# The seam between the key/value stage and the attention loop: an earlier first query chain, with memory of its own and doubly staged weights

## The reference, cut to what matters

```python
# layer 1: cross attention over 16 batches of 128 rows, width 512, 16 query heads, 4 key/value heads of 128
q = layernorm(x) @ Wq + bq ;  k = ctx @ Wk + bk ;  v = ctx @ Wv + bv
q = rmsnorm(q) * qn_w      ;  k = rmsnorm(k) * kn_w           # per head
probs = softmax(q @ k.T / sqrt(128) + mask)                    # each key head serves 4 query heads
x = x + (probs @ v) @ Wo
# layer 2: routed FFN. The best 16 of each batch's 128 rows by a router score are gathered,
# pass an attention block and an MLP, and are scattered back, gated
x = x + ffn(layernorm(x))
```

## Time and profile before

| | |
|---|---|
| median of 3 runs | 876.07 us (873.81 to 878.23) |
| profiled execution, its own time | 879.73 us |
| its span, first to last instruction | 878.0 us |
| TensorE busy | 820.9 us, 93% |
| VectorE, ScalarE, GpSimd busy | 66%, 54%, 53% |
| mean granted TensorE clock | 0.977 of full speed |
| transfers | 81.37 MB, 93 GB/s over the span |
| TensorE waiting in 107 to 155 us | seven waits of 0.76 to 3.74 us |

### The profile page before, as it was taken

One profiled execution on the slowest core, in us unless ns is written; L12 is line 12 of the kernel. 1 busy time (PEld: TensorE's weight loads), 2 busy tenths in 40 slices (PEclk: granted clock), 3 DMA queues, 4 the chain that ended last, 5 costly groups with the idle time before them and its releaser, 6 DMA issues. The chain is left out here.

```text
span 878.0 us, 14307 instructions
## 1 busy us (share of the span) xinstructions
PE 820.9 (93%) x4216; PEld 683.7 (78%) x4216; DVE 577.5 (66%) x1049; ACT 474.0 (54%) x1620; POOL 464.0 (53%) x485
## 2 busy tenths in 40 slices
PE   6999958999999999999999999999987799978997
PEld 4888836888888888888888888888875677766786
DVE  4454445677777777777777777777677588663513
ACT  4555534565566566566566566566554256553431
POOL 2333324555555555555555555555557196644980
PEclk9999997999999999999999999999998699999999
DMA  6566654011111111111111111111024565303520
GB/s 206 202 203 204 202 180 135 13 61 36 48 60 36 48 60 36 48 60 36 48 60 36 48 60 36 48 60 36 24 90 140 213 182 178 118 29 117 192 97 24
DMA packets 49287, 81.37 MB, mean 93 GB/s; under 512 B 4144, under 2 KB 12464, under 8 KB 49264
## 3 DMA queue, kind: packets, MB, share of 16 engines
q1 hardware_dynamic: 48688, 79.25, 27.5%
q0 software_dynamic: 576, 1.84, 0.6%
HBM read 63.77 MB, written 17.30 MB: 92 GB/s over the span
## 5 line engine op out<-in xcount | busy, mean ns | idle before, releaser
L1002 ACT ACTIVATE sq_junk<-q_row 128x128 bf16<-128x128 f32 x256 | 76.0, 298 | 159.6 <-DVE q_row L1256 159.6
L849 POOL TENSOR_TENSOR wp_lo<-raw,wp_hi 128x2048 fp32r<-128x2048 f32 (+1 forms) x24 | 105.0, 4385 | 45.3 <-ACT wp_hi L914 45.2
L1010 ACT ACTIVATE p_row<-s_row,neg_max 128x128 f32<-128x128 f32 x256 | 99.9, 392 | 37.0 <-DVE neg_max L1277 36.4
L1656 PE MATMUL b_y<-wo_hi,oT_hi 128*128 128x512 f32 x256 | 107.1, 419 | 1.0 <-DVE oT_lo L1187 1.0
L1656 PE MATMUL b_q<-wq_hi,xT_hi 128*128 128x512 f32 x252 | 105.6, 419 | 2.2 <-DVE k_row L1210 2.2
L780 POOL TENSOR_TENSOR p_row<-p_row,p_inv 128x512 f32<-128x512 f32 x64 | 66.6, 1041 | 66.7 <-DVE p_inv L1286 66.7
L1658 PE MATMUL b_y<-wo_hi,oT_lo 128*128 128x512 f32 x256 | 101.7, 397 | 0.0
L1657 PE MATMUL b_y<-wo_lo,oT_hi 128*128 128x512 f32 x256 | 101.6, 397 | 0.0
L1658 PE MATMUL b_q<-wq_hi,xT_lo 128*128 128x512 f32 x252 | 99.7, 396 | 0.0
L1657 PE MATMUL b_q<-wq_lo,xT_hi 128*128 128x512 f32 x252 | 99.6, 395 | 0.0
L738 POOL TENSOR_TENSOR q_rs<-q_ss,eps_head 128x4 f32<-128x4 f32 x64 | 12.7, 199 | 153.8 <-ACT sq_junk L1002 153.8
(11 more groups left out here) (298 smaller groups left out, 2266.0 us busy)
## 6 DMA issues: line engine op xcount, KB each, us to landing
cx<-in_ctx_dram SPq DMA_DIRECT2D x16, 256.0 KB, 2.6
wq_raw<-in_L_xattn_Wq_dram SPq DMA_DIRECT2D x16, 256.0 KB, 2.8
wo_raw<-in_L_xattn_Wo_dram SPq DMA_DIRECT2D x16, 256.0 KB, 3.1
v_store<-v_out SPq DMA_DIRECT2D x16, 256.0 KB, 3.3
k_store<-k_out SPq DMA_DIRECT2D x16, 256.0 KB, 2.0
xr<-in_x_dram SPq DMA_DIRECT2D x16, 256.0 KB, 2.7
k_raw<-k_store SPq DMA_DIRECT2D x16, 256.0 KB, 2.6
v_raw<-v_store SPq DMA_DIRECT2D x16, 256.0 KB, 2.8
```

Source lines behind the costliest of these rows:

```text
L849: pool.tensor_tensor(wp_lo[n % NSLOT][:, part, :], raw[RAW_OF[n]][:, part, :], wp_hi[n % NSLOT][:, part, :].bitcast(fp32), ALU.subtract).t ...
L1002: sq = act.activation(sq_junk[:, h, :], q_row[:, h, :], ACT.Square, accum_out=q_ss[:, h:h + 1])
L1010: e = act.activation(p_row[:, h, :], s_row[:, h, :], ACT.Exp, bias=neg_max[:, h:h + 1], accum_out=p_sum[:, h:h + 1])
L1656: pe.matmul(dst, left[0], right[0], start=start, stop=False)
```

## The change

What it does, engine by engine:

- Memory: the query rows, their squares buffer and sums, and `q_nrm` get room of their own, outside what is laid over; the squares of the keys share that buffer; two FFN tiles (`proj`) are put in `q_row` and `q_nrm`. The weight buffers become two slices each of `raw[0]` and `raw[1]`, so two heads can be staged.
- SyncE: loads of head b+1 are issued in batch b, head 0 and 1 both in batch 0, after the splits of Wk and Wv that free the slices. x of batch 0 is loaded in batch 13, not 14. The first quad's bias is issued after the last key projection; then the stores of batch 14, the rest of the query bias, and after the last value projection keys 0, mask, values 0, x of batch 1, residual, last stores. The loop of the queue is written out.
- TensorE: x is turned ahead of key projection 15, query 0 is projected (into `b_y`) between keys 15 and values 15; then keys 15 are turned (into `b_pT`) and quad 1 is projected into `b_q`. In the loop's first batch quad 2 is projected behind scores 0 (into `b_y`), quad 3 behind the turn of quad 1, and the turn of quad 2 has no projection behind it.
- VectorE: statistics of x ahead of the last context split; x normalised between key rows 14 and value rows 14; bias of query 0 between key rows 15 and the low halves of head 15, which now stand ahead of value rows 15; bias 1 before the loop, together with waits for the whole query bias and the mask; bias 2 behind the maxima of quad 0.
- ScalarE: squares of query 0 behind the weighing of keys 14, ahead of the copies of head 15; values 0 copied before the exponentials of quad 0.
- GpSimd: root of x's statistics ahead of keys 14; norm of query 0 right behind keys 15.

```diff
@@ -177,6 +177,13 @@
         f_ms = sb_in(ctx, "f_ms", [P, 2 * NJ])
         f_rs = sb_in(ctx, "f_rs", [P, 2 * NJ])
         raw = [sb_in(ctx, f"raw{i}", [P, 4, W]) for i in range(2)]
+        q_row = sb_in(ctx, "q_row", [P, QUAD, HD])
+        q_nrm = sb_in(ctx, "q_nrm", [P, QUAD, HD])
+        sq_junk = sb_in(ctx, "sq_junk", [P, QUAD, HD], bf16)
+        q_ss = sb_in(ctx, "q_ss", [P, QUAD])
+        q_rs = sb_in(ctx, "q_rs", [P, QUAD])
+        wq_raw = [raw[0][:, i, :].rearrange("p (c d) -> p c d", c=DC) for i in range(2)]
+        wo_raw = [raw[1][:, i, :] for i in range(2)]
 
 
...
@@ -263,7 +262,7 @@
             rope = [sb_in(st, "rope0", [P, 4 * (HD // 2)])]
             onehot = sb_in(st, "onehot", [P, NB, PICK])
 
-            proj = [sb_in(st, f"proj{i}", [P, W]) for i in range(2)]
...
+            def load_x(b):
+                sp.dma_start(xr[:], x_rows[bass.ds(b * S, S), :]).then_inc(x_loaded, 16)
+
+            for b in range(NB - 1):
+                if b < NB - 2:
                     sp.wait_ge(c_turned, b + 1)
-                    sp.dma_start(cx[par][:], ctx_rows[bass.ds((b + 2) * S, S), :]
-                                 ).then_inc(cx_loaded[par], 16)
-
-                wait(sp, w_lo, 2 * b)
-                sp.dma_start(wq_raw[:], chunked(Wq)[:, :, bass.ds(b * HD, HD)]).then_inc(wq_loaded, 16)
-                sp.dma_start(wo_raw[:], Wo[bass.ds(b * P, P), :]).then_inc(wo_loaded, 16)
-                if beside is not None:
-                    beside()
-                if not first:
+                    sp.dma_start(cx[b % 2][:], ctx_rows[(b + 2) * S:(b + 3) * S, :]
+                                 ).then_inc(cx_loaded[b % 2], 16)
+                if b == 0:
+                    load_weights(0)
+                load_weights(b + 1)
+                if b == NB - 3:
+
+                    sp.wait_ge(c_turned, NB - 1)
+                    load_x(0)
+                if b > 0:
                     store_v(b - 1)
                     store_k(b - 1)
...
+            key_weights_over(sp)
+            spread(bq_row[:, 0:W], bq[0:W]).then_inc(first_bias_loaded, 16)
+            store_v(NB - 2)
+            store_k(NB - 2)
+            spread(bq_row[:, W:NH * HD], bq[W:NH * HD]).then_inc(kv_bias_loaded, 16)
...
-            sp.wait_ge(k_stored, 16 * (NB - 1))
-            sp.wait_ge(v_stored, 16 * (NB - 1))
+            sp.wait_ge(k_stored, 16 * (NB - 2))
+            sp.wait_ge(v_stored, 16 * (NB - 2))
+            weights_over(sp)
             load_k(0)
+            sp.dma_start(mask[:], attn_mask.rearrange("a s t -> (a s) t")).then_inc(const_loaded, 16)
             load_v(0)
-            spread(bq_row[:, W:NH * HD], bq[W:NH * HD]).then_inc(kv_bias_loaded, 16)
-            sp.dma_start(x_res[:], x_rows[0:S, :]).then_inc(res_loaded, 16)
-
             sp.wait_ge(x_normed, 1)
             load_x(1)
+            sp.dma_start(x_res[:], x_rows[0:S, :]).then_inc(res_loaded, 16)
             store_v(NB - 1)
             store_k(NB - 1)
...
-            with pool.Fori(0, NB - 1) as b:
+            with pool.Fori(0, NB - 2) as b:
                 kv_batch(b)
 
             def x_norm_stat(b):
@@ -790,11 +787,10 @@
 
 
             x_norm_stat(0)
+            kv_batch(NB - 2)
             kv_batch(NB - 1)
-
-            pool.wait_ge(w_lo, 2 * NB)
+            q_norm(0)
             weights_over(pool)
-            q_norm(0)
             k_low(0)
...
+            def kv_batch(b, par, nth, first, last):
+                if not last:
+                    turn_c(b + 1, 1 - par)
+                act.wait_ge(k_biased, b + 1)
+                wait(act, k_rooted, b)
+                for h in range(NKV):
+                    sq = act.activation(sq_junk[:, h, :], k_row[:, h, :], ACT.Square, accum_out=k_ss[:, h:h + 1])
+                sq.then_inc(k_squared, 1)
+                if not first:
+                    weigh_k(b - 1)
+                if last:
+                    act.wait_ge(k_squared, NB)
+                    squares(0)
+                act.wait_ge(head_loaded[par], 32 * nth)
+                copy(wq_hi[:, :, bass.ds(b * HD, HD)], wq_raw[par]).then_inc(w_hi, 1)
+                copy(wo_hi[:, bass.ds(b, 1), :], wo_raw[par].unsqueeze(1)).then_inc(w_hi, 1)
+
+            kv_batch(0, 0, 1, True, False)
+            with act.Fori(0, NB // 2 - 1) as g:
+                kv_batch(2 * g + 1, 1, g + 1, False, False)
+                kv_batch(2 * g + 2, 0, g + 2, False, False)
...
+            weigh_k(NB - 1, b_pT)
             weights_over(act)
-            weigh_k(NB - 1)
-            squares(0)
             k_high(0)
...
+                    if first and i == 0:
+                        v_high(0)
...
+            x_statistics(0)
+            dve.wait_ge(x_stats, 1)
+            x_moments(0)
+
+            turn_c(NB - 1, 1)
+            key_rows(NB - 2)
+            dve.wait_ge(c_turned, NB)
+            x_norm(0)
+            value_rows(NB - 2)
+            x_low(0)
+            weights_low(NB - 2, 0)
+
+            key_rows(NB - 1)
+            dve.wait_ge(first_bias_loaded, 16)
+            q_bias(0, 0, b_y)
+            weights_low(NB - 1, 1)
+            value_rows(NB - 1)
             weights_over(dve)
-
-            dve.wait_ge(w_lo, 2 * NB)
-            dve.wait_ge(rows_loaded, 32)
-            q_bias(0, 0)
-
             dve.wait_ge(kv_bias_loaded, 48)
+            q_bias(1, 1)
+            dve.wait_ge(const_loaded, 64)
...
-                        q_bias(1, 1, b_y)
                         q_low(0)
...
                     if not (first and i == 0) and not (last and i == NQUAD - 1):
-                        q_bias(t + 1, (i + 1) % NQUAD)
+                        if not (first and i == 1):
+                            q_bias(t + 1, (i + 1) % NQUAD)
                     s_mask(t)
                     s_sum(t)
                     s_max(t)
+                    if first and i == 0:
+                        q_bias(2, 2, b_y)
                     if not (first and i == 0):
                         p_low(t - 1)
...
-            def kv_batch(b, par, next_nth, first=False, last=False):
-                if not last:
+            def kv_batch(b, par, next_nth, first=False, between=None):
...
                 if not first:
                     turn_k(b - 1)
+                if between is not None:
+                    between()
                 wait(pe, v_biased, b)
                 kv_project(b_v, par, wv_hi, wv_lo, DC if first else None).then_inc(v_projected, 1)
-                if last:
-
-                    turn_x(0)
...
-            def project_q(t, b, quad, bank=b_q):
+            def project_q(t, b, quad, bank=b_q, banks=1):
                 pe.wait_ge(xT_lo_done, b + 1)
-                if bank is b_q:
-
-                    wait(pe, q_biased, t)
+                wait(pe, q_biased, t + 1 - banks)
...
-            pe.wait_ge(w_lo, 2 * QUAD)
-            pe.wait_ge(k_biased, NB)
-            project_q(0, 0, 0)
-            turn_k(NB - 1)
+            def first_query():
+                pe.wait_ge(w_lo, 2 * QUAD)
+                project_q(0, 0, 0, b_y, banks=2)
+
+            pe.wait_ge(c_lo, NB)
+            turn_x(0)
+            kv_batch(NB - 1, 1, None, between=first_query)
 
             pe.wait_ge(w_hi, 2 * NB)
             pe.wait_ge(w_lo, 2 * NB)
 
-            project_q(1, 0, 1, b_y)
-
-            pe.wait_ge(k_weighted, NB)
+            pe.wait_ge(k_biased, NB)
+            turn_k(NB - 1, b_pT)
+            project_q(1, 0, 1, banks=2)
             pe.wait_ge(v_biased, NB)
 
             def attend(b, first, last):
@@ -1813,9 +1814,14 @@
                         pe.wait_ge(xT_lo_done, NB)
                         find_places(0)
                     turn_q(t)
-                    if not (first and i == 0) and not (last and i == NQUAD - 1):
+                    if first and i == 1:
+                        project_q(3, 0, 3, banks=2)
+                    if not (first and i < NQUAD - 1) and not (last and i == NQUAD - 1):
                         project_q(t + 1, b if i < NQUAD - 1 else b + 1, (i + 1) % NQUAD)
                     score_quad(t, b, i)
+                    if first and i == 0:
+                        project_q(2, 0, 2, b_y, banks=2)
+                        pe.wait_ge(k_weighted, NB)
                     if not (first and i == 0):
                         turn_p(t - 1)
```

113 lines of the change are left out of this document (39 added, 74 removed).

## The result

The changed kernel takes 871.08 us (median of 8 runs, 867.71 to 874.25), the kernel before in the same runs 877.5 (873.81 to 881.96): a ratio of 0.992, interval 0.9903 to 0.9937. By that ratio 7.0 us of 877.5 are won, between 5.5 and 8.5 (the medians alone differ by 6.4), where 10.5 were forecast; 871.08 lies 1 us above the range's upper end. The direction was right, the size was not.

What follows compares the result with a forecast made beforehand. TensorE bounds the kernel, with about 17 us not work in the seam between key/value stage and attention loop; 12.2 us earlier less 1.7 for one clock drop gives 10.5, so 876.07 becomes 865.6 us, range 862.5 to 870.

Steps and rivals of the forecast that it cites:

- The layout of the sum: TensorE's new order laid out from 107.06 to the fourth quad's turn at 142.5, 12.2 us earlier if the clock stays up.
- the wait for head 15: Before the turn of keys 15: TensorE, ready at 116.28, waits 1.6 us for head 15's weights, until 117.9.
- turn to scores: Quad 0 in the first loop batch: 2.2 us from turn to scores through ScalarE and VectorE, 1.6 of it wait.
- turn to mix: Mix 0 in the first loop batch: nothing put between turn and mix, so 2.99 us stays.
- quad 2: Before scores 2: its projection is used up by drawing forward, so a bare round trip of 2.4 us.
- The rest of the bias: Query bias transfer (768 KB): issued about 114.3, lands between 117.8 and 122.5, taken as 119.5, needed at 121.2.
- the rival of late transfers: Mask or first keys take the full 8.2 us, clock down twice: gain 6.2, 869.9 us; chance 0.18.
- the loop passes on what it is given: Attention loop: it is full, so what TensorE reaches earlier at the fourth quad comes off the end.
- The prediction's own test: If the fourth quad starts 10 us earlier and the span is not 10 us shorter, the loop claim is wrong.
- So I count one drop, 1.7 us: Behind mix 0: one stretch at half clock, costing 1.7 us of the 12.2 us gain.
- rows and keys: 107.06 to 110.60: x's turn, key projection 15, turn of keys 14; x's earlier load and statistics hidden, cost 0.
- both slow stretches of the seam before: Old seam at 134.3 to 138.1 and 144.5 to 148.4: lower clock costing 1.9 and 1.7 us.

Runs made afterwards that it cites:

- warm_all: Changed kernel with the store of values 12 ahead of x's load and idle-time matmuls in the seam and behind the loop: 864.08 us, ratio 0.9831.
- the pair with fillers: Kernel before and changed kernel, each with the same 53 idle-time matmuls behind the loop alone: 874.39 against 866.32 us.
- memory_alone: Kernel before with only the change's memory layout, one weight buffer each, order of work as before: 877.69 us, ratio 0.9992.
- before_ffnwarm: Kernel before with 53 idle-time matmuls behind the loop alone: 874.39 us, ratio 0.9964.
- store_ffnwarm: Changed kernel with the store of values 12 ahead of x's load and idle-time matmuls behind the loop alone: 867.22 us, ratio 0.9879.
- loop_as_before: Changed kernel with the first loop batch in its old order, quads 2 and 3 not drawn forward: 871.22 us, ratio 0.9922.
- before_warm: Kernel before with idle-time matmuls in the waits of its own seam and behind the loop: 871.92 us, ratio 0.9928.
- the bias alone: Kernel before with the rest of the query bias issued right behind the mask: 879.66 us, ratio 1.0016.
- values_first: Changed kernel with TensorE alone put back to project values 15 before query 0: 875.77 us, ratio 0.9967.

## Why the prediction missed its range

**Right.** The layout of the sum. At full clock it has 142.5 - 104.23 = 38.3 us from values 14 to the fourth quad; warm_all, where the clock is held up and x is not late, has 38.5. Term by term in the changed kernel's profile: the wait for head 15 1.41 (the start of the turn at 118.27, 117.9 forecast), turn to scores 2.25 (2.2), turn to mix 2.99 (2.99), quad 2 2.23 (2.4). The rest of the bias, the mask and keys 0 were there in time, and the rival of late transfers did not happen. The rest of the bias was issued at 115.08 and took 4.9 us to land, 120.0 where 119.5 was forecast. That is partly luck: of the bounds in the earlier trace rows 3.5 us is the first quad's bias of 256 KB and 8.2 the rest of 768 KB, so the low end was read from a transfer of a third of the size. That the loop passes on what it is given is shown by the pair with fillers: 7.4 us at the seam, 7.3 in the spans of the same executions. The prediction's own test looks worse in the first two profiles, where the fourth quad is 9.0 us earlier and the span 6.4 shorter. Of the difference 0.6 lies in the loop and 2.0 behind the last query turn (231.9 us instead of 229.9); but that part varies with the clock in the same kernel (229.9 and 227.7 before), and with fillers in it the kernels of both orders have 224.2 to 225.8.

**Wrong, first: "So I count one drop, 1.7 us".** The mechanism was right, in the place forecast, the size of this term was not. I took 1.7 from one stretch of 3.9 us of the kernel before, and for that kernel it was nearly right: from mix 0 to the fourth quad it took 11.35 and 11.39 us with the drop, and 9.45 and 9.48 where the drop did not come (memory_alone, before_ffnwarm), 1.9 less. The same size did not hold for the new order. There the stretch takes 8.47 to 8.49 us in the three profiles with the clock held up and 10.77 to 12.28 in the seven without. So a drop costs 2.3 to 3.8 there, not 1.7; in whole time 3.1 separate warm_all from store_ffnwarm. In the changed kernel it begins ahead of scores 2 and the lower level lasts over the 5.35 us that follow; in the second profile it begins at mix 0. With the old order of these quads put back (loop_as_before) the stretch took 11.24, 1.8 over the 9.45: the drop became dearer with the order that leaves quad 2's wait bare behind mix 0's. The rule that the prediction cites from the Trainium skill (TensorE: Matmul & The Clock Gate, section "Loop structure matters more than you think"), that a VectorE copy out of PSUM doesn't let the array go cold, would by the prediction's reading have given 12.2. The changed kernel's row of 137.75 to 143.10 at 0.50 speaks against that reading: two waits for VectorE, of 2.38 and 1.64, with one mix and one turn between, were followed by the lower level, here and in the second profile. The pattern that this section of the Trainium skill shows has the next matmuls follow immediately, which they did not do here.

**Wrong, second: "Cost 0" for rows and keys.** I followed the load of x for when x would be there, and not what stands behind it in the queue. It was moved ahead of the store of values 12; VectorE's value rows 13 wait for that store, some 1.1 us longer, and x's statistics stand behind them on VectorE. x's turn then stood 0.2 to 0.7 us. This is worth up to 0.9 in a seam (39.44 against 38.49). The trace of the kernel before already held the price: x's load is ahead of a store there one batch later, and its value rows came 4.4 us after the issue of the store, against 3.4 in the batch ahead (98.43 to 101.79). The kernel before:

```profile
105.30 0.43 SPq L547 DMA_DIRECT2D v_store<-v_out  x1
109.71 0.69 DVE L1214 TENSOR_TENSOR v_out<-b_scores,bv_row 128x512 f32<-128x512 f32 x1 [4.44 <-DMA v_store<-v_out]
```

**Third, smaller.** The loop's 0.4 us from the tiles' places, priced at 0. And the sum took both slow stretches of the seam before, 3.6 us, as winnable; before_warm shows 1.2 to 2.5, and the second of them is missing in two of the five profiles that have the old seam without fillers.

Together: 10.5 less 0.6 to 2.1 for the clock, 0.2 to 0.9 for x, 0.4 for the loop leaves 7.1 to 9.3, and up to 1.9 less where the kernel before runs without its own drop; the pair with fillers has 8.1, the plain comparison 7.0 with 5.5 to 8.5. What lies between 7.0 and 8.1 is within the noise of the plain one, whose runs spread with the clock behind the loop (867.71 at a mean clock of 0.985 and 874.25 at 0.980 are its ends). The range was too narrow above because inside it late transfers were the only way to lose and the size of a drop was held for known.

**Parts that do nothing by themselves.** Drawing two projections forward (loop_as_before) and the memory (memory_alone) measure as 0, the bias alone as a loss of 1.4 us or nothing, though at another place in the queue than the change's. At least half of the gain hangs on one order, query 0 ahead of the values (values_first: 4 to 5 us of the time). Not shown: what the staging of two heads is worth, since no run has the new order with one head staged, and what the queue's new order is worth by itself.

## What to carry to other kernels

When a transfer is moved in a queue, follow the instruction that waits for whatever is now behind it, on its engine, to the end; a load of 256 KB ahead of a store made the rows that wait for the store 1.1 us later here, and the load's own data is used behind them. A wait is not only its own length: two short ones close together took TensorE to 1.2 GHz and cost 2.3 to 3.8 us of work behind them, more than the 1.9 that a drop at that place cost in the old order, and matmuls that nobody reads, counted a little under each wait and put into a bank that is free, gave that back (15 us of 877 in all, with the changed order). Where runs spread by more than the effect, hold that clock up in both kernels and compare those.
